# A weights' part and the first attention steps: transfers of keys placed later in the queue, stores awaited in the next part, part of the queries' products first, and a loop written out

## The reference, cut to what matters

```
x = x + attention0(layernorm(x), ctx)          # 16 heads, softmax over 128 keys, temperature
x = x + ffn0(layernorm(x))                      # 512 -> 2048 -> 512, weights and activations quantised, relu
x = x + attention1(layernorm(x), ctx)           # 16 heads, no softmax, then a layernorm of its own
x = x + tanh(((layernorm(x) @ W) @ A1) @ A2 + b)
```

## Time and profile before

| | us |
|---|---|
| runs, lowest / median / highest (3) | 1885.74 / 1889.35 / 1894.01 |
| the profiled execution, its own time | 1883.58 |
| its span | 1881.8 |

### The profile page before, as it was taken

How to read it: one execution, slowest core, us unless ns; L and a number is a source line. 1 busy time by engine, 2 the same in 40 slices (tenths; PEclk the granted TensorE clock), 3 DMA queues, 4 the chain that set the end, 5 groups by cost and what they waited for, 6 DMA issues and landing times. The chain is left out here.

```text
span 1881.8 us, 31634 instructions
## 1 busy us (share of the span) xinstructions
PE 1797.2 (96%) x9447; PEld 1350.0 (72%) x9530; DVE 1548.8 (82%) x3607; ACT 1237.9 (66%) x3379; POOL 952.4 (51%) x1053
## 2 busy tenths in 40 slices
PE   8996899999999999999879999889999999999997
PEld 7785688888888888888744444366677767767775
DVE  6756789999989999998769888888888888888875
ACT  4554899999989999999733333356555555555543
POOL 3120456666666666666520000156766666667664
PEclk9998999999999999999989999999999999999999
DMA  8368334454454444433369999164445445444311
GB/s 290 135 202 241 72 96 113 129 125 113 113 132 124 113 113 128 126 91 91 90 219 386 396 397 396 51 225 160 158 151 196 148 158 198 149 156 170 120 52 40
DMA packets 146944, 308.63 MB, mean 164 GB/s; under 512 B 44496, under 2 KB 56784, under 8 KB 129104
## 3 DMA queue, kind: packets, MB, share of 16 engines
q1 hardware_dynamic: 146624, 306.26, 50.4%
q10 hardware_dynamic: 144, 0.26, 0.1%
HBM read 165.95 MB, written 106.95 MB: 145 GB/s over the span
## 5 line engine op out<-in xcount | busy, mean ns | idle before, releaser
L1240 POOL TENSOR_TENSOR a_pr<-a_pr,a_rcp 128x512 f32<-128x512 f32 x256 | 266.4, 1041 | 286.2 <-DVE a_rcp L1086 285.8
L999 ACT ACTIVATE a_pr<-a_s,a_nmax 128x128 f32<-128x128 f32 x1024 | 364.0, 380 | 18.8 <-DVE a_nmax L1079 17.1
L1489 PE MATMUL f_pair<-f_room,w 128*128 128x512 bf16 x999 | 223.9, 381 | 2.6 <-ACT f_room L1600 1.3
L999 ACT ACTIVATION_READ_ACCUMULATOR a_pr<-a_s,a_nmax 128x1 f32 x1024 | 224.3, 219 | 0.0
L1931 POOL TENSOR_TENSOR f_ring<-f_ring,f_room 128x512 f32<-128x512 f32 x64 | 82.0, 1281 | 244.3 <-DVE f_room L1876 244.3
L1712 DVE CUSTOM_DVE_ANT_0 f_hf<-f_pair,nb,sh 128x512 f32<-128x512 f32 x244 | 172.0, 748 | 29.0 <-PE f_pair L1489 23.5
L1079 DVE TENSOR_REDUCE a_nmax<-a_s 128x4 f32<-128x512 f32 x256 | 173.6, 678 | 16.6 <-PE a_s L892 16.5
L1094 DVE TENSOR_TENSOR a_pTl<-a_pt,a_pTh 128x512 fp32r<-128x512 f32 x256 | 168.6, 679 | 18.1 <-ACT a_pTh L1008 17.2
L1489 PEld LDWEIGHTS f_pair<-f_room,w 128*128 128x128 bf16 x1024 | 99.2, 98 | 115.8 <-issue 2.1
L1644 ACT ACTIVATE f_room<-f_ring,f_off,f_rs 128x512 f32<-128x512 f32 x128 | 104.0, 812 | 115.0 <-POOL f_off L1922 114.1
L1916 POOL TENSOR_TENSOR f_rs<-f_rs,f_half 128x1 f32<-128x1 f32 x128 | 72.0, 562 | 187.2 <-DVE f_rs L1765 187.2
(11 more groups left out here) (392 smaller groups left out, 5150.0 us busy)
## 6 DMA issues: line engine op xcount, KB each, us to landing
hidden<-f_hf SPq DMA_DIRECT2D x57, 1024.0 KB, 9.6
f_hf<-hidden SPq DMA_DIRECT2D x57, 1024.0 KB, 5.2
xb<-x SPq DMA_DIRECT2D x16, 1024.0 KB, 5.6
a_qs<-bqreph SPq DMA_DIRECT2D x128, 128.0 KB, 2.3
a_qs<-bqrepl SPq DMA_DIRECT2D x128, 128.0 KB, 2.4
a_xr<-x SPq DMA_DIRECT2D x64, 256.0 KB, 3.8
x<-a_xr SPq DMA_DIRECT2D x64, 256.0 KB, 2.5
f_ring<-x SPq DMA_DIRECT2D x64, 256.0 KB, 4.8
```

What stands on the lines that cost most here:

```text
L999: last = e.activation(pr[:, t, j, :], s_bank[t][:, j * P:j * P + P], ACT.Exp, bias=nmax[kk % 2][:, t, j:j + 1], accum_out=sums[kk % 2][:, ...
L1240: e.tensor_tensor(p, p, rcp[kk % 2][:, t, :].unsqueeze(2).to_broadcast([P, 4, KEYS]), ALU.mult).then_inc(*e_pn)
L1489: last = e.matmul(h_bank[(PAIRS * u + i) % 3][:, q, :], w1[:, k, f * P:f * P + P], xT[u % 2][:, k, :], start=k == 0, stop=k == KC - 1)
```

## The change

Five edits. In prepare, SP's call keys() is split: eight transfers (the first two groups of KEY_ROWS) now stand behind the pieces send_m(3, range(KC)), ahead of load 19, and the last four behind the last piece of m, ahead of send_w2(3). The stores of wc signal a semaphore of their own (e_wc), and the wait for them leaves the end of prepare; ACT waits for them in attend, at its first phi. In attend, PE's queries(b, kk, 0) stands ahead of scores(b, kk, 0) in the steps kk = 1 to 4 of the first batch too. The loop over batches 1 and 2 becomes straight code on every engine. In rest, two semaphores are merged into one, with the same waits.

```
@@ prepare, SP @@
-            def keys():
-                e_clear.wait_ge(e, 0)
-                for c in range(KC):
-                    e_send[c].wait_ge(e, 3)
-                for dst, h, at in KEY_ROWS:
+            def keys(rows_of_keys):
+                for dst, h, at in rows_of_keys:
...
             send_w2(0)
-            keys()
             send_w2(1)
             load(16)
             load(17)
             load(18)
             send_m(3, range(KC))
+            e_clear.wait_ge(e, 0)
+            for c in range(KC):
+                e_send[c].wait_ge(e, 3)
+            keys(KEY_ROWS[:2])
             load(19)
             load(20)
             send_w2(2)
             send_m(3, (KC,))
+            keys(KEY_ROWS[2:])
             send_w2(3)
             load(21)
             for i in range(KC):
                 e_gone.wait_ge(e, by_dve[place["wc"][i]])
                 for h in range(2):
-                    e.dma_start(scr["wc"][h, :, i, :], f32(outs[i][h][:])).then_inc(*e_send[i])
+                    e.dma_start(scr["wc"][h, :, i, :], f32(outs[i][h][:])).then_inc(scr["e_wc"].sem, 16)
             load(22)
             for i in range(4):
-                e_send[i].wait_ge(e, 5)
                 e_mout[i].wait_ge(e, 4)
@@ body_steps @@
-    with e.Fori(1, NB - 1) as b:
+    for b in range(1, NB - 1):
         for kk in range(per):
             fn(b, kk)
@@ attend, PE's step @@
+                early = first(b) and 0 <= kk < WO
+                if early:
+                    queries(b, kk, 0)
                 if opening:
-                    queries(b, kk, 0)
                     queries(b, kk, 1)
                 scores(b, kk, 0)
                 pt(b, kk, 0)
-                if not opening:
+                if not early:
                     queries(b, kk, 0)
@@ attend, ACT's phi @@
                 e_pt.wait_ge(e, 4 * (b * TPB + o) + t)
+                if first(b) and (o, t) == (0, 0):
+                    scr["e_wc"].wait_ge(e, 0)
```

More of the change, by code:

```diff
@@ L1434, in rest @@
         e_top2, e_all2, e_hscale, e_s2 = ev("top2"), ev("all2"), ev("hiddenscale"), ev("s2")
-        e_half, e_pick, e_zero, e_r2 = (ev(n) for n in ("half", "pick", "zero", "row2"))
+        e_half, e_pick, e_r2 = (ev(n) for n in ("half", "pick", "row2"))
         e_xc, e_fb = ev("xc"), ev("fb")
@@ L1565, in last_ffn @@
                 last.then_inc(*e_f)
-            e_pick.wait_ge(e, 1)
+            e_pick.wait_ge(e, 2)
             e_w.wait_ge(e, 10)
@@ L1662, in _ @@
                 if u == 7:
-                    e_zero.wait_ge(e, 0)
+                    e_pick.wait_ge(e, 0)
                 if u in (8, 9, 10, 11):
@@ L1902, in _ @@
                 last = e.memset(f32(r[:]), 0.0)
-            last.then_inc(*e_zero)
+            last.then_inc(*e_pick)
             e.memset(f32(pick[:]), 0.0).then_inc(*e_pick)
-            e_pick.wait_ge(e, 0)
+            e_pick.wait_ge(e, 1)
             e.memset(f32(pick[0:1, :]), 1.0)
             e.memset(f32(pick[32:33, :]), 1.0).then_inc(*e_pick)
-            e_pick.wait_ge(e, 1)
+            e_pick.wait_ge(e, 2)
             e_half.wait_ge(e, 0)
@@ L2091, in program @@
             scr["e_x"] = [Event(scr["sem"](f"xload{i}"), 16) for i in range(2)]
+            scr["e_wc"] = Event(scr["sem"]("wcout"), 16 * 2 * KC)
             kept = nc.snapshot_sems()
```

3 lines of the change are left out of this document (1 added, 2 removed).

## The result

| | before | after |
|---|---|---|
| median of four runs of each, us | 1888.76 | 1873.9 |
| lowest to highest | 1885.74 to 1894.01 | 1873.07 to 1874.97 |
| ratio, 95% interval | | 0.9914 (0.9899 to 0.9929) |
| the profiled execution, its own time | 1883.58 | 1874.35 |
| its span | 1881.8 | 1872.6 |

The kernel is 14.9 us faster at the median, more than the 0.5% that can be told from no change. The two profiled executions differ by only 9.2 us. The one of before, at 1883.58, was shorter than every other run of that kernel in this document (the lowest of them is 1884.54).

A forecast was written before the change was run, and what follows sets the result against it. Attention's long stretches were taken as full on PE, so only the weights' part's end, attention's first steps and the loop's jump could move: -8.2 - 1.0 + 0.5 + 1.5 - 4.6 = -11.8, giving 1877.6 us, range 1869 to 1887.

The forecast's parts named there:

- part 1: End of the weights' part: keys moved behind the last matrix's pieces let DVE end 8.2 us earlier, bounds -6.2 and -9.4.
- part 2: Attention's start: no wait for wc's last stores, -1.0 us; first a_qs transfers queueing behind load 22, +0.5.
- part 3: Attention's steps 1 to 4: queries ahead of scores delay phi(0) and the exponentials, +1.5 us, bounds -0.3 and +4.5.
- part 4: Loop's jump back: straight code removes what two steps there take over plain ones, -4.6 us, bounds -5 and -3.5.
- Load 16 and the chain behind it: Weights' part: load 16 issued at 126.9 instead of 133.65, landing near 134.0; load 19 out at 146.7.
- The rival of a queue full again: Weights' part: the eight moved keys cost 11.3 us instead of 5.2, giving 1883.6; chance 0.17.
- Weight 9: End of the weights' part: load 21, issued at 156.7, lands at 163.9 and is hidden; at 166.4, 2 us less gained.
- signs of being wrong: Profile after: keys over 1 us each, weight 9 waiting for load 21, half clock in steps 1 to 4, plain steps over 11.6.
- The last stores: Between DVE's end and attention's start: dropping SP's wait for wc's last store gains between 0 and 1.7 us, taken as -1.0.
- The queries' transfers behind load 22: Attention's first a_qs transfers queue behind load 22 and the last stores: between 0 and 1.4 us, taken as +0.5.
- the clock as a rival: Attention's first steps: later scores leave longer gaps and cost the clock, +4.2 us in four steps, giving 1881.8; chance 0.15.
- The slower rival: The 32 steps written out: straight code not fetched in time, up to 1.06 us more each, giving 1911.5; chance 0.03.

The follow-up runs named there:

- a_w2late: The changed kernel with the two last stores, send_w2(2) and send_w2(3), placed behind load 21; 1874.59 us, ratio to before 0.9921.
- a_load22: The changed kernel with load 22 (1 MB of tokens) issued behind attention's first transfers of queries; 1874.08 us, ratio to before 0.9919.
- keys_only: The kernel before with only the calls of keys() split and moved as in the change; 1885.4 us, ratio to before 0.9987.
- a_nokeys: The changed kernel with the twelve transfers of keys back in their old place, ahead of load 16; 1879.41 us, ratio to before 0.9944.
- a_loop: The changed kernel with the loop over batches 1 and 2 back on all five engines; 1883.01 us, ratio to before 0.9976.
- a_noq: The changed kernel with the old order of PE's queries in steps 1 to 4; 1876.94 us, ratio to before 0.9933.
- a_best: The changed kernel with both last stores behind load 21, load 22 behind the first a_qs, DVE's stats(1) and norm(1) later; 1871.39 us, ratio to before 0.9913.

## Why the prediction came out as it did

The forecast was 1877.6, 11.8 less; measured was 14.9 less, inside the range. That it lay so near is in part luck: errors of both signs in the terms. In the pair of profiles, which the terms were worked out for, part 1 came as -5.4 (-8.2 forecast), part 2 as +0.6 (-0.5), part 3 as -1.1 (+1.5) and part 4 as -4.0 (-4.6), with +0.7 elsewhere: 9.2 less. At the medians the loop, and perhaps the order of the queries, brought more than that.

**Load 16 and the chain behind it: right.** Issue at 126.25 (126.9 forecast), DVE's maximum at 132.80 (134.0), keys at 140.50 (141.2), load 19 at 146.15 (146.7), ACT at 151.64 (152.5), halve wc 3 at 164.97 (165.7). The rival of a queue full again fell for the eight keys: 5.60 us, where it had 11.3. That all transfers run on the same 16 DMA engines (the Trainium skill, DMA: Bandwidth & Descriptors, Issuing engines are not separate DMA queues), so that moving the keys saves none of their time, didn't decide here; their order in SP's list did.

**Weight 9: the step that failed in part 1.** "At 7.2, as load 16 with the same store ahead, it lands at 163.9 and is hidden." The load was issued at 158.99, not 156.7, and took 8.1. DVE then waited 3.36 us ahead of weight 9, which was one of the signs of being wrong that I had named. The term was -5.4, not -8.2, outside its bounds of -6.2 and -9.4. I had counted the transfers moved ahead of load 21 and their free price, but not the state of the queue there: the full queue of the rival did come, seven us later than where I looked. The held piece itself ended at 155.76, no later than weight 8's buffer was free (153.59 + 2.29 = 155.88); what made load 21 late were the 3.1 us of four keys and a store still to be issued behind it. The profile of before had a row for it. SP in time, before, 154 to 160:

```profile
154.94 4.57 SPq L675 DMA_DIRECT2D m_all<-p_stage  x1
```

The same piece, with load 20 and the same store ahead of it, was held for 4.57 us. It cost nothing there since nobody waited, and so I passed over it. a_w2late shows that the store makes the difference.

**The last stores: -1.4, -1.0 forecast. The queries' transfers behind load 22: +2.0, +0.5 forecast.** Together +0.6 instead of -0.5. I had bounded the second by 1.4, the time by which DVE's chain is shorter. But load 22 was issued 5.4 us ahead of the first a_qs, more than before (4.6). What decided was how much the 16 DMA engines still had to do. Busy time by stretch, before, with the DMA share as the last number but one:

```profile
172.00:174.00 2.00, 2.00 (x10) 1.66 (x9) 1.65 (x4) 2.00 (x2) 0.00 (x0) 1.00 0.45 137
```

The same stretch of after, where the first queries are issued:

```profile
172.00:174.00 2.00, 1.70 (x4) 1.45 (x5) 0.00 (x0) 0.00 (x0) 0.60 (x4) 0.50 1.06 435
```

In after load 22 lands at 177.74, 10.9 us behind its issue, and the first a_qs at 177.79, right with it. That fits the same 16 engines being busy with the load; that a_qs stood behind it in SP's own queue fits as well, and no run separates the two. a_load22 shows the load as the cause, keys_only that the removed wait bought nothing at the scores.

**The order of the queries: +1.5 forecast; -0.9 alone and -3.0 in company, neither clear of the noise.** The mechanism that I described is there: plain steps 0.1 to 0.3 longer, step 0 longer too. What I left out is that the steps ran with stretches at half clock before, which cost 1.6 each and which the new order, with the keys moved, has in only two of seven profiles. I had the clock as a rival with the opposite sign.

**The loop: mis-sized.** -4.6 forecast; -7.7 alone, 9.1 when taken back from the full change. The hole of 3.41 us and the step behind it were read rightly from a profile in which the jump was the cheapest of six. That this execution lay 5.8 below its own median was in the text, and I carried the difference over as if no term depended on it. The slower rival (straight code not fetched in time) fell: plain steps take 11.54.

By the runs, then, taken out of the full change: keys 5.5 (a_nokeys), loop 9.1 (a_loop), queries 3.0 (a_noq), more than 14.9. From the ratios instead of the medians they are 5.7, 11.7 and 3.6, of 16.2. Added alone they bring 2.9, 7.7 and 0.9, together 11.5. Each of the first carries an error of about 3 us, and the runs of after were all made in one session; so the medians don't show that the edits depend on one another. The profiles do in one place: keys and order of the queries together are in five of seven profiles without the half-clock stretches that each alone has.

**Open:** what makes steps of 12 us away from the jump, where the scatter of the runs comes from, and what makes the clock fall in one early step and not in the next. The moved wait and the merged semaphore had no run of their own; from the last tile's first maximum on, where the merged semaphore lies, both profiles take 960.8 us.

## What to carry to other kernels

A transfer's place in the issuing queue is worth what waits behind it. When you move transfers, follow every later load past them, and read for each neighbour how long its issue was held before, also where nobody waited for it. A term that belongs to a rare event (a jump, a clock stretch) wants several executions: a profile below its own median may be cheap in exactly such terms, as the jump was here. And when one wait goes, work out the next two; here load, bank and clock stood behind one another within 2 us.

## What the runs showed of the hardware

- SP issues a transfer of 64 KB in 0.6 to 0.7 us. With two loads of 1 MB and a store of 512 KB in 256-byte packets just issued, the next transfer of 256 KB was held for 7.6 to 8.3 us in seven profiles; with the two loads alone ahead, its issue took 0.43 (a_w2late, a_best).
- A loop's jump back on PE, ACT, DVE and POOL together, once, cost 3.4 to 4.7 us of standing DVE, 5.1 us over two steps on average, and 7.7 to 9.2 us of the median. SP's jump alone cost 3.9, with some 3 us of error.
- A load of 1 MB took 10.9 us to land while the DMA engines' share was at 1, and the transfers behind it landed with it.
- The end of one block and the start of the next cost 0.3 us when no transfer was waited for (171.98 to 172.27).
- A step with 3.4 us at half clock in it took 12.9 us, where the steps beside it took 11.3.
